# A gated cross-attention block with a routed expert layer on one core: an own order for the last groups of tiles, scatters beside the counting, gathers ahead of register loads, and the mix in 29 products

## The reference

```python
xn = layernorm(layernorm(x), ln_gamma, ln_beta)
q, (k, v) = xn @ w_q, split(ctx @ w_kv)
attn = softmax(q k^T / 8)                      # 16 heads x 77 keys
x = x + tanh(g_xattn) * tanh(gate) * (attn v @ w_out + b_out)
y = layernorm(x)
probs = softmax(y @ gate_w.T + gate_b)         # 10 gates
weights, selected = top_k(probs, 2)            # gates 8, 9: no expert
out = sum over the true choices of norm_w * (y @ expert_w[e] + expert_b[e])
x = x + tanh(g_ffn) * out
```

## Time and profile before

| what | us |
|---|---|
| median of three runs (1550.4 to 1561.01) | 1552.9 |
| the profiled execution's own time | 1539.97 |
| its span, first to last instruction | 1538.2 |
| TensorE busy | 1336.4 |
| VectorE busy | 1204.0 |
| GpSimd busy | 921.5 |
| ScalarE busy | 785.8 |

### The profile page before, as it was taken

One profiled execution on the slowest core, in us unless ns is written; L12 is line 12 of the kernel. 1 busy time (PEld: TensorE's weight loads), 2 busy tenths in 40 slices (PEclk: granted clock), 3 DMA queues, 4 the chain that ended last, 5 costly groups with the idle time before them and its releaser, 6 DMA issues. The chain is left out here.

```text
span 1538.2 us, 31337 instructions
## 1 busy us (share of the span) xinstructions
PE 1336.4 (87%) x7241; PEld 685.0 (45%) x7242; DVE 1204.0 (78%) x2764; ACT 785.8 (51%) x2777; POOL 921.5 (60%) x781
## 2 busy tenths in 40 slices
PE   5676199999999999999999999998039998899997
PEld 4332054444444444444444444544015554455553
DVE  5766478899999999999999999996356775666765
ACT  5766266655555555565555555554024443344442
POOL 0450255557666766766776776674537775666664
PEclk9787699999999999999999999999569999999999
DMA  5795468889887788887788987777135442677773
GB/s 199 195 241 166 136 128 179 179 189 217 180 238 163 179 191 215 213 195 171 172 206 198 235 182 167 172 155 174 63 131 169 161 155 101 212 239 238 238 235 116
DMA packets 419892, 280.37 MB, mean 182 GB/s; under 512 B 325009, under 2 KB 352785, under 8 KB 419448
## 3 DMA queue, kind: packets, MB, share of 16 engines
q1 hardware_dynamic: 391992, 205.52, 55.1%
q0 software_dynamic: 27840, 74.18, 15.3%
HBM read 123.38 MB, written 83.07 MB: 134 GB/s over the span
## 5 line engine op out<-in xcount | busy, mean ns | idle before, releaser
L752 PE MATMUL scores<-m_sb,zT 128*128 (+2 forms) x2304 | 416.4, 339 | 43.3 <-DMA zT<-z_parts 31.2
L768 PE MATMUL mix<-u_sb,pT 128*128 128x512 f16 (+1 forms) x1920 | 425.0, 379 | 0.6 <-DVE x_out L947 0.6
L841 ACT ACTIVATE expd<-scores,less 128x77 f32<-128x77 f32 x1024 | 317.4, 329 | 203.4 <-DVE less L923 202.5
L1582 PE MATMUL out_bank<-w_parts,y_columns 128*128 x1440 | 335.7, 384 | 2.3 <-issue 2.2
L752 PEld LDWEIGHTS scores<-m_sb,zT 128*128 128x128 f16 x2304 | 223.6, 98 | 212.1 <-DMA zT<-z_parts 31.6
L768 PEld LDWEIGHTS mix<-u_sb,pT 128*128 128x128 f16 (+1 forms) x1920 | 187.8, 98 | 220.5 <-DVE x_out L947 0.8
L841 ACT ACTIVATION_READ_ACCUMULATOR expd<-scores,less 128x1 f32 x1024 | 213.9, 209 | 0.0
L1582 PEld LDWEIGHTS out_bank<-w_parts,y_columns 128*128 128x128 f16 x1440 | 142.2, 99 | 152.2 <-issue 13.6
L1247 POOL DMA_INDIRECT table<-payload,row_i x128 | 158.6, 1239 | 59.2 <-issue 34.7
L1605 ACT CAST y_columns<-yT_bank 128x512 f16<-128x512 f32 x120 | 70.2, 585 | 183.9 <-PE yT_bank L1569 183.9
L1224 POOL TENSOR_TENSOR z<-z,beta 128x512 f32<-128x512 f32 x64 | 152.0, 2376 | 5.0
(11 more groups left out here) (158 smaller groups left out, 1880.1 us busy)
## 6 DMA issues: line engine op xcount, KB each, us to landing
comb<-x_out SPq DMA_DIRECT2D x64, 512.0 KB, 3.2
x_ln<-in_x_dram SPq DMA_DIRECT2D x64, 256.0 KB, 2.7
x_res<-in_x_dram SPq DMA_DIRECT2D x64, 256.0 KB, 2.8
w_raw<-in_L_ffn_expert_w_dram SPq DMA_DIRECT2D x64, 128.0 KB, 2.3
m_dram<-m_stage SPq DMA_DIRECT2D x32, 231.0 KB, 5.7
u_dram<-m_sb SPq DMA_DIRECT2D x48, 154.0 KB
m_sb<-m_dram SPq DMA_DIRECT2D x12, 616.0 KB
u_sb<-u_dram SPq DMA_DIRECT2D x6, 1024.0 KB, 6.8
```

Of the source, the lines that this page charges most:

```text
L752: last = pe.matmul(scores[s][k][:, 0:n], zT[:, s, zp, t, :], m, start=(t == 0 and (zp, mp) == PRODUCTS[0]), stop=(t == DT - 1 and (zp, mp) ...
L768: last = pe.matmul(mix[:], pT[0:n, s, pp, k, :], u_sb[0:n, k, up, :], start=(k == 0 and (pp, up) == PRODUCTS[0]), stop=(k == KT - 1 and (p ...
L841: last = act.activation(expd[:, s, h * KEYS:(h + 1) * KEYS], scores[s][k][:, at:at + KEYS], ACT.Exp, bias=less[:, s, h:h + 1], scale=1.0 / ...
L1582: last = pe.matmul(c.out_bank[s][:], yT[:, s, yp, t, :], w_parts[:, bass.ds(e, 1), t, wp, :].rearrange("p a n -> p (a n)"), start=(t == 0 ...
```

## The change

The mix's last block of rows, 80 of 128, took three products; now the 48 rows that were padding hold the products of the high probabilities with the low half of `u`, so two products do: 29 a tile. For this ScalarE copies 48 more columns of high probabilities and VectorE 32 more, ahead of their large ones, and the stores and loads of `u`'s last block become more and smaller DMAs. The eleven extra steps become four `tail` steps with an order of their own, in which group 14 is routed one tile earlier, and group 14 has a second `payload` and `row_i`. The eight scatters of group 15 move from the end of `attend` into `list_tiles`, where SyncE waits for them before it loads the table; the bias is loaded first. The iotas move to the start of `attend`, and the zeroing of the rings moves from GpSimd to ScalarE. In `run_experts` the first token numbers and the first four gathers come ahead of the register loads. The core of the diff:

```diff
+ROOM = P - LAST
+LAST_LO = LAST + (LAST - ROOM)
...
     yield engine.dma_start(u_sb[:, k0:whole], u[k0 * P:whole * P].rearrange("(k p) l n -> p k l n", p=P))
     if k1 == KT:
-        yield engine.dma_start(u_sb[0:LAST, KT - 1], u[(KT - 1) * P:COLS])
+        first = (KT - 1) * P
+        yield engine.dma_start(u_sb[0:LAST, KT - 1], u[first:COLS, 0:1].broadcast_to([LAST, 2, D]))
+        yield engine.dma_start(u_sb[LAST:P, KT - 1, 0], u[first:first + ROOM, 1])
+        yield engine.dma_start(u_sb[LAST:LAST_LO, KT - 1, 1], u[first + ROOM:COLS, 1])
...
             if b > 0:
-                return [(slice(0, KEYS), u_dram[b, h * KEYS:(h + 1) * KEYS])]
+                return [(stage, u_dram[b, h * KEYS:(h + 1) * KEYS])]
             k, row = divmod(h * KEYS, P)
             fit = min(KEYS, P - row)
-            pieces = [(slice(0, fit), u_sb[row:row + fit, k])]
-            if fit < KEYS:
-                pieces.append((slice(fit, KEYS), u_sb[0:KEYS - fit, k + 1]))
+            pieces = []
+            for k, row, j0, j1 in ((k, row, 0, fit), (k + 1, 0, fit, KEYS)):
+                if j0 == j1:
+                    continue
+                end = row + j1 - j0
+                if k < KT - 1:
+                    pieces.append((stage[j0:j1], u_sb[row:end, k]))
+                    continue
+                hi = stage[j0:j1, 0:1].broadcast_to([j1 - j0, 2, D])
+                pieces.append((hi, u_sb[row:end, k]))
+                split = min(end, ROOM)
+                pieces.append((stage[j0:j0 + split - row, 1], u_sb[LAST + row:LAST + split, k, 0]))
+                if split < end:
+                    pieces.append((stage[j0 + split - row:j1, 1], u_sb[LAST:LAST + end - split, k, 1]))
             return pieces
...
-            for i in range(last, TILES + 2 * GROUP + 3):
+            for i in range(last, TILES):
                 step(i, i % 2, i // GROUP, i % GROUP)
+            for i in range(TILES, TILES + GROUP):
+                tail(i, i % 2, i % GROUP)
...
+        def side(g):
+
+            return 1 if isinstance(g, int) and g == GROUPS - 2 else 0
...
-                        pe.wait_ge(u_in[g], (32 if k1 == KT else 16) * (i // TPB))
-                    for k in range(k0, k1):
-                        n = P if k < KT - 1 else LAST
+                        pe.wait_ge(u_in[g], (64 if k1 == KT else 16) * (i // TPB))
+                    for k in range(k0, min(k1, KT - 1)):
                         for pp, up in PRODUCTS:
-                            last = pe.matmul(mix[:], pT[0:n, s, pp, k, :], u_sb[0:n, k, up, :],
-                                             start=(k == 0 and (pp, up) == PRODUCTS[0]),
-                                             stop=(k == KT - 1 and (pp, up) == PRODUCTS[-1]))
+                            last = pe.matmul(mix[:], pT[:, s, pp, k, :], u_sb[:, k, up, :],
+                                             start=(k == 0 and (pp, up) == PRODUCTS[0]), stop=False)
+                    if k1 == KT:
+
+                        for part, n in ((0, P), (1, LAST_LO)):
+                            last = pe.matmul(mix[:], pT[0:n, s, part, KT - 1, :], u_sb[0:n, KT - 1, part, :],
+                                             start=False, stop=(part == 1))
                     if k1 < KT:
                         last.then_inc(u_read, 1)
...
+            def tail(i, s, turn):
+                if live(i - 2):
+                    mix_values(i - 2, s)
+                if i == TILES + 1:
+                    pe.wait_ge(place_ready, GROUPS - 1)
+                gate(i - 4, s, GROUPS, turn)
+                if i == TILES:
+                    rank(GROUPS - 2)
+                if i == TILES + GROUP - 1:
...
+                act.copy(p_parts[:, 0, COLS:], expd[:, s, (KT - 1) * P:(KT - 1) * P + ROOM])
                 act.copy(p_parts[:, 0, 0:COLS], expd[:, s, :]).then_inc(p_hi_ready, 1)
...
+                dve.tensor_copy(p_parts[:, 1, COLS:COLS + LAST_LO - LAST], p_parts[:, 0, COLS - (LAST_LO - LAST):COLS])
                 dve.tensor_tensor(p_parts[:, 1, 0:COLS], expd[:, s, :], p_parts[:, 0, 0:COLS],
...
-                    dve.wait_ge(scattered, 16 * GROUP * TOP_K * g)
+                    dve.wait_ge(scattered, 16 * GROUP * TOP_K * (g - side(g) - side(g - 1)))
...
+                    listing.scatter(pool, table, side(g), t, k)
+
+            def tail(i, s, turn):
+                ps, t = 1 - s, (i - 3) % GROUP
+                if live(i - 3):
+                    y_rstd(i - 3, ps, t)
+                    y_low(i - 3, ps)
+                if i == TILES:
+                    scatter(GROUPS - 3, ((1, 0), (1, 1), (2, 0)))
+                if i == TILES + 1:
+                    scatter(GROUPS - 3, ((2, 1), (3, 0), (3, 1)))
+                    scatter(GROUPS - 2, ((0, 0), (0, 1)))
+                if i == TILES + 2:
...
-            run(pool, step)
-            pool.wait_ge(scattered, 16 * TOP_K * TILES)
+            pool.iota(listing.iota_j[:], pattern=[[RING, PASSES], [1, LISTED], [0, EXPERTS]], base=0,
+                      channel_multiplier=0, allow_small_or_imprecise_dtypes=True)
+            pool.iota(listing.iota_r[:], pattern=[[0, TOP_K], [RING, PASSES]], base=0, channel_multiplier=0,
+                      allow_small_or_imprecise_dtypes=True)
+            run(pool, step, tail)
...
+            sp.dma_start(expert_bias[:], expert_b.rearrange("(a e) d -> a e d", a=1).broadcast_to(
+                [P, EXPERTS, D])).then_inc(bias_in, 16)
+
+            sp.wait_ge(listing.scattered, 16 * TOP_K * TILES)
             for k in range(TOP_K):
                 half = slice(k * TABLE_TILES // TOP_K, (k + 1) * TABLE_TILES // TOP_K)
                 sp.dma_start(table_sb[:, half], table.rearrange("(p t) w -> p t w", p=P)[:, half]).then_inc(
                     table_in[k], 16)
-            sp.dma_start(expert_bias[:], expert_b.rearrange("(a e) d -> a e d", a=1).broadcast_to(
-                [P, EXPERTS, D])).then_inc(bias_in, 16)
             sp.wait_ge(bias_in, 16)
...
-            pool.iota(iota_j[:], pattern=[[RING, PASSES], [1, LISTED], [0, EXPERTS]], base=0, channel_multiplier=0,
-                      allow_small_or_imprecise_dtypes=True).then_inc(iotas, 1)
-            pool.iota(iota_r[:], pattern=[[0, TOP_K], [RING, PASSES]], base=0, channel_multiplier=0,
-                      allow_small_or_imprecise_dtypes=True).then_inc(iotas, 1)
-            for ring in got_rings:
-                pool.memset(ring[:], 0.0)
+            for t in range(GROUP):
+                for k in range(TOP_K):
+                    listing.scatter(pool, table, 0, t, k)
+            for ring in got_rings:
+                n = RING * D if len(ring.shape) == 3 else 2 * RING * D
+                flat = ring[:].rearrange("p s d -> p (s d)") if n == RING * D else ring[:].rearrange(
+                    "p s l d -> p (s l d)")
+                act.activation(flat, ones16[:, 0:1].broadcast_to([P, n]), ACT.Copy, scale=0.0)
...
+            for j in range(LEAD):
+                gathers(choices[0], j, j)
...
+            for j in range(R):
+                name_token(choices[0], 0, j, j)
```

More of the change, by code:

```diff
@@ L408, in attend @@
 def attend(nc, ident16, x_in, ln_gamma, ln_beta, m_dram, u_dram, m_sb, u_sb, comb, gate_w, gate_b,
-           g_ffn, table, placed, ones16, expert_w, w_parts):
+           g_ffn, table, placed, ones16, expert_w, w_parts, listing):
     with ExitStack() as stack:
@@ L573, in live_group, with run @@
             return not isinstance(g, int) or 0 <= g < GROUPS
-        def run(engine, step):
+        def run(engine, step, tail):
             first, last = 3 * GROUP, TILES - GROUP
@@ L820, in step @@
                     gate(i - 4, s, q, turn)
-            run(pe, step)
+            def tail(i, s, turn):
[7 more added lines that the diff above has]
+                if i == TILES + GROUP - 1:
+                    rank(GROUPS - 1)
+            run(pe, step, tail)
         @block.scalar
@@ L891, in _ @@
             act.activation(g_tanh[:], g_raw[:], ACT.Tanh).then_inc(g_ready, 1)
-            run(act, step)
+            run(act, step, tail)
         @block.vector
@@ L1211, in _ @@
             dve.wait_ge(placed_ready, 1)
-            run(dve, step)
+            run(dve, step, tail)
         @block.gpsimd
@@ L1393, in _ @@
             dve.wait_ge(starts_ready, 1)
-            dve.wait_ge(iotas, 2)
             for k in range(TOP_K):
@@ L1453, in run_experts @@
     EARLY = 4
+    LEAD = 4
     TURNS = 3
@@ L1548, in step @@
                         gather(choices[1].got[s], two_ring[:, s, 0], halves, early_x[:, s, :])
-                    if live(4):
-                        _, place, j = at(r, s, 4)
+                    if live(LEAD) and not (c.k == 0 and isinstance(r, int) and s + LEAD < LEAD):
+                        _, place, j = at(r, s, LEAD)
                         gathers(c, place, j)
@@ L1554, in step @@
                         scatter(c, place, j)
-                tiles = run(pool, c, step, 4)
```

(8 more changed lines are left out.)

116 lines of the change are left out of this document (99 added, 17 removed).

## The result

The changed kernel takes 1545.76 us (median of 20 runs, 1540.28 to 1553.37) against 1553.65 us before (20 runs beside it, 1549.86 to 1562.2): ratio 0.9945, 95% interval 0.9931 to 0.9958, so 8.5 us less by the ratio; the two medians lie 7.9 us apart. Forecast were 1546.7 us and 6.2 us less; 1553.65 is 0.75 us over the median that the forecast started from. The gain is under 1%, but the interval does not reach 1.

A forecast was written before the change was run, and what follows sets the result against it. VectorE was taken to bound the attention loop, with TensorE within 1%. Terms 2.5 + 7.8 - 1.1 - 13.5 - 1.9 = -6.2 us, carried over to the runs' median of 1552.9, gave 1546.7 us; range 1528 to 1559.

The forecast's parts named there:

- stores of `u`: Stores of the context's values for batch 0 become 28 instead of 25 and delay VectorE's restart: +2.5 us, bounds 0 and 5.
- VectorE's copy: Attention loop: VectorE's 128x32 copy ahead of `low_p` costs 0.13 us a tile, +7.8 us over 60 tiles.
- mix at the end: From about tile 59, where VectorE waits for TensorE, five mixes each save one 0.221 us matmul: -1.1 us.
- tail and list: After the attention loop: earlier routing of group 14 and counting under the scatters bring the finished list forward, -13.5 us.
- gathers ahead: Start of `run_experts`: first token numbers come after the block's boundary, 0.6 us, without the register load: -1.9 us.
- The ring: Attention loop: VectorE's work plus a short piece of ScalarE form a closed circle without TensorE, 13.8 us a tile.
- The packed columns: Attention loop: the copy costs 0.08 us in three turns of four, 0.28 where it lets GpSimd's beta go first.
- The tail: Last groups' routing: the 8.65 us wait before the last payload goes; two scatters ahead of the last `x_moments` cost 2.6.
- rival C: Tail gives back less: a 2.94 us gap falls between the last eight scatters; gain 7.6, not 13.5; 1552.6 us; chance 0.15.
- Counting beside the scatters: VectorE's sums, 15.5 us at most, run under the last scatters and finish by 1105, three us before the table.
- A: TensorE bounds the attention loop after all, so packing pays in every tile: -27.0 us, 1525.9 us; chance 0.12.
- B: Attention loop: the copy costs VectorE the port every turn, 16.8 us, total 1555.7; strong form near 1620; chance 0.13 (strong 0.02).

The follow-up runs named there:

- the light `w_parts`: Changed kernel, low half of expert weights made for one column of 256: 1524.65 us with 30 products and no packing, 1531.7 us with 29.

## Why the prediction was right

The forecast was the likeliest case, within 1%, and the median lies 0.9 us from it. The sum is less good than that looks:

| step | forecast | in the rows |
|---|---|---|
| stores of `u` (one pair of profiles) | +2.5 | +0.5 |
| VectorE's copy | +7.8 | +9.3 |
| mix at the end | -1.1 | -0.1 |
| tail and list | -13.5 | -10.0 |
| gathers ahead | -1.9 | -2.0 |
| sum | -6.2 | -2.3 |

Counted to the first `biased` (1.1 us more) and without the stores it is the -3.9 us of the table above. 4.6 us of the measured 8.5 are not in these rows: the sum came 4 us short of the gain that I forecast, and what the rows don't hold made up for it. That the number is so close is in part luck.

*What bounds the loop.* Right: a product less per tile gave TensorE waits and no time, and the packing alone was slower. The ring was drawn too small: GpSimd's chain and its turns at the port belong to it, as the light `w_parts` showed. TensorE's slack was read too small as well: of its waits before, 200 to 1035 us, I took the 4.4 us of the earlier trace rows and left out

```profile
PE scores L752 <- ACT expd L841: 7.1, 12, 0.7
```

It was idle for 27 of those 835 us, 3% and not 1%. Neither changes the forecast.

*The packed columns.* Right in mechanism and place: three turns of 0.08 (0.07 to 0.09), one larger turn, the one with `logits`, where beta goes first. The term for that one was mis-sized, 0.41 us and not 0.28: I followed the flip over `low_p` and `w_parts`, where it costs next to nothing, and not on to `z_parts`, which comes forward by 0.8 us onto `less`. From the first to the 64th reciprocal it is 860.6 - 851.3 = 9.3 us.

*The stores.* Mis-sized. There are 28 in 23.7 us, as forecast, but VectorE restarted only 0.14 us later for it. SyncE's queue and VectorE after:

```profile
106.29 23.74 SPq L283 DMA_DIRECT2D u_sb<-m_sb  x28
```

```profile
133.65 16.74 DVE L407 SCALAR_TENSOR_TENSOR m_sb<-fold,u_gain,m_sb 77x512 f16<-77x512 f32 x25 [2.71 <-ACT m_sb L382]
150.62 11.76 DVE L407 SCALAR_TENSOR_TENSOR m_sb<-fold,u_gain,m_sb 77x512 f16<-77x512 f32 x17 [0.23 <-ACT m_sb L382]
```

The restart is 27.36 us behind the first store, before 27.22. The three extra stores belong to the last heads of batch 0 and stand at the end of that row. The 0.23 us of idle time at 150.62 is not theirs: before has 0.28 us there too. From the first store to the end of those to DRAM it is 56.8 us against 56.3, the +0.5 of the table, and even that is not the stores' for sure: over all profiles the stretch is 55.4 to 56.5 us with 25 stores and 55.6 to 56.8 with 28. The term should have been nothing.

*The mix at the end.* Mis-sized. From the last reciprocal to the last `x_out` the time went from 17.25 to 17.12 us only.

*The tail.* Right in kind. "Two more scatters ahead of the last x_moments" were counted at 1.28 us each; I gave the gap of 2.94 us to rival C alone, between the last eight. It fell instead ahead of `x_moments`, where it delays the whole chain: `x_moments` starts 7.0 us after the last `x_out` and not 4.6. That is 2.4 of the 3.5 us that the tail and the list fell short. From the table's first load to the finished `slots` it was 15.3 us (1109.40 to 1124.73) where I took 14.4, and one of the last eight scatters held GpSimd 0.8 us longer than the rest; some 0.5 us lie between `x_moments` and the first of the eight; the last scatter's landing gave 1.1 back (1108.24 to 1109.40, not 2.3).

*Counting beside the scatters* and *first gathers ahead*: right; counting was done at 1105.36 with the table issued at 1109.40, and the boundary's 0.6 was 0.56 us. The iotas cost nothing to be seen: from the last store of `u` to the first reciprocal it is 35.8 us, before 37.0.

*The rivals.* A is excluded by the packing alone. B came true in one turn of four and not in the others, as the case I took said. C's gap was real, its place other than I put it.

## What to carry to other kernels

Where VectorE and GpSimd take turns at SBUF, follow a shift of 0.1 us through the whole turn: look which instruction of the other engine moves and what it then meets, since shortening an instruction is worth little while it stands behind another's turn. A matmul saved on an engine that waits, by as little as 3% of its time, gave nothing here, and the instruction that paid for it on the ring cost 9.3 us in 63 turns, nearly twice the 0.08 us a turn that it takes where nothing else shifts; put such a helper on the engine with slack (here ScalarE: 9 us back). And where one gap in a queue is unexplained, expect it ahead of the same DMA in the changed order and price it on the path it will then stand on.

## What the runs showed of the hardware

The gap on GpSimd's queue moves with its DMA and not with what stands around it. In all 14 profiles (two of before, two of after, one of each other kernel) it stands ahead of the 114th indirect DMA of the kernel, and a second of 2.8 us ahead of the 233rd, 119 later. In the three with the two scatters later the first is 1.7 us instead of 2.9 to 3.1. The 114th is in every order the second scatter of group 14, so that these runs don't tell whether the gap belongs to the count or to that scatter. What the queue does there is open.

A VectorE instruction on one column took 1.23 us behind GpSimd's beta. And the expert layer, the same code, took 383 to 385 us in some profiles and 396 to 405 in others. The nine long ones hold 25 to 52 us of waits of ScalarE and VectorE whose releaser the profile does not know, the five short ones none. The four profiles of the comparison in which before took 1537.58 us are all short, the eight of the other two comparisons all long: which of the two a run showed went by the occasion, not by the kernel.
